# Adding the first heads' maxima to the transposed scores by matmuls, in a two-layer decoder on one core

## The chip, the core and the metric

The kernel runs on one core of one Trainium2 chip. The metric is the device time of one execution in microseconds (us); the median of several runs counts.

## The reference

Two decoder layers on x of 8 x 128 tokens x 128 features. Each layer is attention, cross attention and a mixture of experts, each with a residual and a layer norm after it. What matters here are the two self-attentions, with heads of width 8:

```
# layer 0: 16 heads, each with two queries and keys (c = 0, 1), differential attention
# layer 1: 16 heads in 8 pairs, causal
score = q @ k.T * 8 ** -0.5            # 128 x 128 for each of 8 sequences
attn  = softmax(score, axis=-1)        # row maximum subtracted, exp, divided by the row sum
y     = attn @ v
x     = layernorm(x + y @ Wout)
```

## The kernel before

**Stages.** The program is one instruction stream for each engine, tied by semaphores. Its stages are: projections and rotary tables of layer 0 (up to 34 us), attention A (layer 0, 16 heads, 34 to 111 us), cross attention, experts of layer 0, projections of layer 1, attention D (layer 1, 8 head pairs, causal, 216 to 269 us), cross attention with 16 heads, and the experts of layer 1 up to the end. A head below is one of the 16 steps of A or one of the 8 of D; each has 16 tiles of 128 x 128 scores (two columns c and 8 sequences b).

**Stacks.** Queries and keys are split in three bfloat16 parts each. The nine products of parts are made in one matmul by stacking: `queries_of[slot]` and `keys_of[slot]` hold 72 rows (`ROWS`: 3 x 3 x 8), read back from DRAM by `load_stacks` with four DMAs a head, into one of 8 slots (`RING`). Semaphore `stack[h % 4]` tells that head h has landed.

**What a head does.** Scores are made twice.

- `scores` (L600) multiplies queries by keys (72 rows) into banks 2 and 3, four tiles to a group g = 0 to 3; VectorE takes the negated row maxima of a group (`maxima`, L1384) and so frees the bank for the group after next.
- GpSimd splits the 16 maxima of each row in three bfloat16 parts (`split_maxima`, L486 to L492, semaphore `msplit`), TensorE transposes them to 48 x 128 (`head_maxima`, L632), ScalarE copies the result into `mT` (`copy_maxima`, semaphore `mc`).
- SyncE then moves `mT` by a DMA into rows 72 to 74 of the queries' stack (`move_maxima`, L368, semaphore `mrow`). Against these rows the keys' stack holds ones, so that
- `scores_t` (L613) makes the transposed scores with the maxima already subtracted, with 75 rows, into banks 4 and 5; ScalarE takes the exponential (`exponentials`), and
- `head_values` (L644) and `head_token` (L656) multiply by the values and transpose back.

In D each group of scores begins with one more matmul that adds the causal mask (L606, L619, 512 columns).

**Order.** TensorE's order is written out by hand in `heads` (L659). Heads 0 and 1 get their scores ahead, with `keep_busy` matmuls (L598, 128 x 512, results unused) in between; the transposition of head 0's maxima is placed inside head 1. Then come groups 0 and 1 of head 2, `keep_busy(8)`, and the steps: step n holds the transposed scores of head n, the scores of head n+2 (groups 2, 3) and n+3 (groups 0, 1), the maxima of head n+1, the values of head n-1. Steps 1 and 2 begin with `keep_busy(4)`. SyncE's order is: load stacks 0 to 3, then for each n: move the maxima of head n, load stack n+4.

Of the kernel before, what the change touches and what calls it, by code (L numbers as in the profile page):

```python
# [22 lines left out]
P = 128  # L23
# [18 lines left out]
RING = 8  # L42
AHEAD = FLIGHT = 4
LOADS = PARTS + 1
ONES_PAIR = 1.0019378662109375
EARLY_VALUES = 4
NEAR_VALUES = 3
# [59 lines left out]
def decoder_kernel(nc, d, out):  # L107
    with ExitStack() as ctx:
        def sb(name, shape, dt=F32):
            return ctx.enter_context(nc.sbuf_tensor(name, shape, dt))  # L110

        def sem(name):
            return ctx.enter_context(nc.semaphore(name))
# [3 lines left out]
        con = sb("con", [P, C_ALL])  # L117
        identb, trib, onesb, causS, causT, minusb = (
            sb(n, [P, P], BF16) for n in ("identb", "trib", "onesb", "causS", "causT", "minusb"))
        one = sb("one", [P, 1])  # L120
        xres = sb("xres", [P, B, P])
        racc = sb("racc", [P, B, P])
# [107 lines left out]
        def tiles(ap, n, w):  # L230
            return ap[:, 0:n * w].rearrange("p (a b) -> p a b", b=w)
# [3 lines left out]
        def over(ap, n):  # L235

            return ap.unsqueeze(1).to_broadcast([ap.shape[0], n, ap.shape[1]])
# [8 lines left out]
        def late_head(n, count):  # L246

            return isinstance(n, int) and n >= count
# [44 lines left out]
                self.y = sem(n + "_y")  # L293

        A, D = Heads("a", 0), Heads("d", NH // FLIGHT)
        ln_var, ln_rstd, ln_out, ln_tp, ln_xT = (sem("ln_" + n) for n in ("var", "rstd", "out", "tp", "xT"))
        resb = sem("resb")
        bkv, bkvc = sem("b_kv"), sem("b_kvc")
# [25 lines left out]
        def _(sp):  # L324
# [39 lines left out]

            def move_maxima(a, n, slot):

                sp.wait_ge(a.mc, n + 1)
                sp.dma_start(queries_of[slot][MROW:MROW + PARTS], mT[:, n % 2, :]).then_inc(a.mrow[n % FLIGHT], 16)  # L368

# [222 lines left out]
        def _(pe):  # L592
            mm = nc.tensor.matmul

            def keep_busy(count, at):

                for _ in range(count):
                    mm(bank(at), onesb[:], fill, start=True, stop=True)  # L598

            def scores(a, n, slot, g, causal):  # L600

                if not early(4 * n + g, 2):
                    pe.wait_ge(a.max, 4 * n + g - 1)
                o = bank(BANK_S + g % 2)
                if causal:
                    mm(tiles(o, 4, P), identb[:], over(causS[:], 4), start=True, stop=False)  # L606
                for k in range(4):
                    c, b = divmod(4 * g + k, B)
                    last = mm(o[:, k * P:(k + 1) * P], queries_of[slot][0:ROWS, c, b * P:(b + 1) * P],  # L609
                              keys_of[slot][0:ROWS, c, b * P:(b + 1) * P], start=not causal, stop=not causal or k == 3)  # L610
                last.then_inc(a.s, 1)

            def scores_t(a, n, slot, g, causal):  # L613

                if not early(4 * n + g, 2):
                    pe.wait_ge(a.exp, 4 * n + g - 1)
                o = bank(BANK_T + g % 2)
                if causal:
                    mm(tiles(o, 4, P), identb[:], over(causT[:], 4), start=True, stop=False)  # L619
                for k in range(4):  # L620
                    c, b = divmod(4 * g + k, B)
                    last = mm(o[:, k * P:(k + 1) * P], keys_of[slot][0:MROW + PARTS, c, b * P:(b + 1) * P],  # L622
                              queries_of[slot][0:MROW + PARTS, c, b * P:(b + 1) * P],
                              start=not causal, stop=not causal or k == 3)
                last.then_inc(a.st, 1)

            def head_maxima(a, n, slot):
# [31 lines left out]
            def heads(a, count, pair, causal):  # L659

                def step(n, slot):
                    ahead, second, third, before = ((slot + k) % RING for k in (1, 2, 3, -1))
                    if not late_head(n, count):
                        if n in (1, 2):
                            keep_busy(4, BANK_O + 1)
                        pe.wait_ge(a.mrow[n % FLIGHT], (a.turns + n // FLIGHT + 1) * 16)
                        scores_t(a, n, slot, 0, causal)
                        scores_t(a, n, slot, 1, causal)
                    if not late_head(n + 2, count):
                        scores(a, n + 2, second, 2, causal)  # L670
                    if not late_head(n + 1, count):
                        head_maxima(a, n + 1, ahead)
                    if not early(n, 1):
                        head_values(a, n - 1, before, pair, 0)
                    if not late_head(n + 2, count):
                        scores(a, n + 2, second, 3, causal)
                    if not early(n, 1):
                        head_values(a, n - 1, before, pair, 1)
                    if not late_head(n, count):
                        scores_t(a, n, slot, 2, causal)  # L680
                        scores_t(a, n, slot, 3, causal)
                    if not late_head(n + 3, count):
                        pe.wait_ge(a.stack[(n + 3) % FLIGHT], (a.turns + (n + 3) // FLIGHT + 1) * 16 * LOADS)
                        scores(a, n + 3, third, 0, causal)
                        scores(a, n + 3, third, 1, causal)
                    if not early(n, 1):
                        head_token(a, n - 1)

                for h in range(2):
                    pe.wait_ge(a.stack[h], (a.turns + 1) * 16 * LOADS)  # L690
                    for g in range(4):
                        scores(a, h, h, g, causal)
                        keep_busy(1 if causal else 2, BANK_O)
                        if h == 1 and g == 1:
                            head_maxima(a, 0, 0)
                pe.wait_ge(a.stack[2], (a.turns + 1) * 16 * LOADS)
                scores(a, 2, 2, 0, causal)
                scores(a, 2, 2, 1, causal)
                keep_busy(8, BANK_O)
                for n in range(count + 1):  # L700
                    step(n, n % RING)

# [93 lines left out]
            keep_busy(10, BANK_M0)  # L796
            pe.wait_ge(bkvc, 4)
            pe.wait_ge(fixed, 8)
            heads(A, NH, pair=False, causal=False)
            finish(A, 2, wproj0)  # L800
            keep_busy(10, BANK_T)
# [292 lines left out]
        def _(act):  # L1094
# [15 lines left out]
            def heads(a, count):  # L1110
                def exponentials(n, slot, g):
                    act.wait_ge(a.st, 4 * n + g + 1)
                    if g == 0 and not early(n, 2):
                        act.wait_ge(a.pv, n - 1)
                    fn(probs[:, slot % 2, 4 * g:4 * g + 4, :], tiles(bank(BANK_T + g % 2), 4, P), ACT.Exp).then_inc(a.exp, 1)

                def copy_maxima(n, slot):
                    act.wait_ge(a.mt, n + 1)
                    if not early(n, 2):
                        act.wait_ge(a.mrow[(n - 2) % FLIGHT], (a.turns + (n - 2) // FLIGHT + 1) * 16)  # L1120
                    fn(mT[:, slot % 2, :], maxima_bank[0:PARTS * 16, :], ACT.Copy).then_inc(a.mc, 1)

                def copy_outputs(n, slot):
                    act.wait_ge(a.pv, n + 1)
                    if not early(n, 1):
                        act.wait_ge(a.to, n)
                    fn(outT[:], bank(BANK_O + slot % 2), ACT.Copy).then_inc(a.ot, 1)

                def step(n, slot):
                    if not late_head(n, count):  # L1130
                        exponentials(n, slot, 0)
                    if not late_head(n + 1, count):

                        copy_maxima(n + 1, (slot + 1) % RING)
                    if not late_head(n, count):
                        exponentials(n, slot, 1)
                    if not early(n, 1):
                        copy_outputs(n - 1, (slot - 1) % RING)
                    if not late_head(n, count):
                        exponentials(n, slot, 2)  # L1140
                        exponentials(n, slot, 3)

                copy_maxima(0, 0)
                for n in range(count + 1):
                    step(n, n % RING)
# [225 lines left out]
        def _(dve):  # L1371
# [3 lines left out]
            def link(ins):  # L1375
                dch(ins)
                dch.wait()
# [103 lines left out]
            dve.wait_ge(lam_exp, 1)  # L1481
            link(tt(lams[:, 4:5], lams[:, 3:4], lams[:, 2:3], ALU.subtract))
            link(ts(lams[:, 5:6], lams[:, 4:5], -(0.8 - 0.6), None, ALU.add))
            heads(A, NH, finish_a)
            for half in range(2):
                dve.wait_ge(A.y, half + 1)
# [297 lines left out]
```

## Time and profile before

| | us |
|---|---|
| median of 3 runs | 510.82 |
| the runs | 511.9, 509.09, 510.82 |
| the profiled execution | 507.72 |
| its span, first to last instruction | 505.6 |

The profiled execution lies 3.1 us below the median of the runs; about 2 us of it lie around the span. The chain of work that ended last is 74% TensorE, 10% VectorE, 7% DMA and 4% ScalarE. The profile names TensorE's matmuls PE and its weight loads PEld. A matmul's row gives its start and a modelled length which contains the pipeline's depth, so matmuls that follow each other overlap in it; the distance from start to start is what one costs. The chain of work shows these costs added up without overlap.

### The profile page before, as it was taken

The numbers are of one execution on the slowest core, as the hardware profiler recorded it, in microseconds if no ns is written. First come the engines' busy times: TensorE is split into PE (matmuls) and PEld (weight loads), VectorE is DVE, ScalarE is ACT, GpSimd is POOL, SyncE is SP. The second block draws the span as 40 slices with busy tenths as digits, with TensorE's granted clock in tenths as the row PEclk, the third lists the DMA queues.
The fourth block names the chain that finished last, engine by engine and source line by source line (L and its number), as shares of the span: only waits on it lengthen the run. The fifth ranks groups of instructions, "written<-read, shape, count | busy, mean of one in ns | idle before, by whom it ended". The sixth has DMA issues, their size and how long they took to land.

```text
span 505.6 us, 11016 instructions
## 1 busy us (share of the span) xinstructions
PE 460.2 (91%) x4144; PEld 331.5 (66%) x4144; DVE 266.6 (53%) x682; ACT 237.7 (47%) x467; POOL 108.5 (21%) x227
## 2 busy tenths in 40 slices
PE   9698999988589998989998899998989999999993
PEld 3165777766345994346677678787866677677773
DVE  4725778716781537654534688876033422333236
ACT  2943667751231423404564588878305434433340
POOL 4202445423200012211111345444010000000001
PEclk9699999999959999989999999999999999999998
DMA  6866455150400000574101000100000011111111
GB/s 173 312 199 156 145 146 153 43 184 17 168 0 1 0 3 6 158 175 118 51 25 49 12 13 17 52 2 1 1 2 21 22 32 42 42 42 32 30 33 42
DMA packets 23307, 34.40 MB, mean 68 GB/s; under 512 B 7600, under 2 KB 16000, under 8 KB 23008
## 3 DMA queue, kind: packets, MB, share of 16 engines
q1 hardware_dynamic: 23264, 33.81, 22.7%
q8 instruction: 30, 0.49, 0.4%
q14 instruction: 13, 0.11, 0.1%
HBM read 28.26 MB, written 5.24 MB: 66 GB/s over the span
## 4 chain that ended last, share of the span: by engine, by line
PE 74%; DVE 10%; DMA 7%; ACT 4%; issue 2%; SPq 1%; POOL 1%; POOLq 0%; DVEq 0%; ACTq 0%
PE ps L1033 11%; PE ps L1050 11%; PE ps L644 4%; PE ps L622 4%; PE ps L609 4%; PE ps L956 3%; PE ps L980 3%; PE ps L598 3%; PE ps L1021 3%; PE ps L967 3%; PE ps L927 3%; PE ps L851 2%; ACT arena L1098 2%; DMA arena<-mT 2%; PE ps L885 2%; PE ps L656 2%
## 5 line engine op out<-in xcount | busy, mean ns | idle before, releaser
L1384 DVE TENSOR_REDUCE negm<-ps 128x4 f32<-128x512 f32 x96 | 64.0, 688 | 36.9 <-PE ps L609 34.7
L1098 ACT ACTIVATE arena<-ps,w1a 128x512 f32<-128x512 f32 x64 | 43.5, 687 | 58.9 <-PE ps L1033 57.8
L1707 DVE SCALAR_TENSOR_TENSOR racc<-ps,sm,racc 128x128 f32<-128x128 f32 x128 | 35.9, 344 | 63.2 <-PE ps L1050 63.1
L1098 ACT ACTIVATE probs<-ps 128x512 f32<-128x512 f32 (+1 forms) x100 | 56.4, 592 | 23.2 <-PE ps L622 22.3
L1050 PEld LDWEIGHTS ps<-w1a,arena 128*128 128x128 f32 x512 | 59.4, 192 | 7.2 <-issue 6.2
L1050 PE MATMUL ps<-w1a,arena 128*128 128x128 f32 x512 | 59.8, 275 | 0.8 <-DVE racc L1698 0.8
L1033 PE MATMUL ps<-xT,w1a 128*128 128x512 f32 x128 | 58.8, 601 | 1.4 <-ACT xT L1098 1.4
L1098 ACT ACTIVATE arena<-ps 128x512 f32<-128x512 f32 (+4 forms) x71 | 40.3, 592 | 35.5 <-PE ps L851 16.1
L533 POOL TENSOR_SCALAR rstd<-mv 128x4 f32<-128x4 f32 x12 | 2.7, 228 | 185.3 <-DVE mv L1430 185.3
L598 PE MATMUL ps<-onesb 128*128 128x512 bf16 x134 | 38.6, 417 | 3.0 <-DVE sm L1562 2.1
L1033 PEld LDWEIGHTS ps<-xT,w1a 128*128 128x128 f32 x128 | 23.1, 191 | 24.6 <-issue 22.2
L577 POOL TENSOR_TENSOR probs<-probs,rzE 128x480 f32<-128x480 f32 x32 | 30.9, 988 | 38.3 <-DVE rzE L1643 38.3
L644 PE MATMUL ps<-probs,vs 128*32 128x128 f32 x768 | 29.7, 278 | 0.7 <-issue 0.7
L1098 ACT ACTIVATE xT<-ps 128x512 f32<-128x512 f32 x10 | 6.0, 596 | 43.9 <-PE ps L729 43.8
L1098 ACT ACTIVATE outT<-ps 128x512 f32<-128x512 f32 x24 | 14.3, 597 | 18.3 <-PE ps L644 18.3
L1098 ACT ACTIVATE probs<-ps,negm 128x120 f32<-128x120 f32 x64 | 17.9, 368 | 10.5 <-DVE negm L1625 10.5
L598 PEld LDWEIGHTS ps<-onesb 128*128 128x128 bf16 x134 | 13.3, 105 | 14.4 <-issue 3.3
L1642 DVE TENSOR_REDUCE rzE<-probs 128x4 f32<-128x480 f32 x32 | 20.3, 635 | 3.8 <-ACT probs L1098 3.8
L1625 DVE TENSOR_REDUCE negm<-ps 128x4 f32<-128x480 f32 x32 | 19.2, 641 | 4.6 <-PE ps L956 4.6
L644 PEld LDWEIGHTS ps<-probs,vs 128*32 128x32 f32 x768 | 18.5, 109 | 4.5 <-issue 1.1
L486 POOL TENSOR_TENSOR mparts<-negm,zero 128x16 bf16<-128x16 f32 x24 | 5.3, 222 | 67.4 <-DVE negm L1384 67.4
L1098 ACT ACTIVATE near<-ps 120x512 f32<-120x512 f32 x32 | 17.5, 604 | 4.2 <-PE ps L967 4.2
(211 smaller groups left out, 816.8 us busy)
## 6 DMA issues: line engine op xcount, KB each, us to landing
stackA<-arena SPq DMA_DIRECT2D x12, 256.0 KB, 3.5
arena<-stackA SPq DMA_DIRECT2D x24, 96.0 KB
arena<-stackA SPq DMA_DIRECT2D x8, 288.0 KB
w1a<-in_w1a SPq DMA_DIRECT2D x1, 2048.0 KB, 8.7
w2a<-in_w2a SPq DMA_DIRECT2D x1, 2048.0 KB, 7.7
w1a<-in_w1b SPq DMA_DIRECT2D x16, 128.0 KB, 2.0
w1a<-in_w2b SPq DMA_DIRECT2D x16, 128.0 KB, 2.0
stackD<-arena SPq DMA_DIRECT2D x6, 256.0 KB
```

Of the source, the lines that this page charges most:

```text
L577: nc.gpsimd.tensor_tensor(weights, weights, along(rzE[:, slot, 4 * g:4 * g + 4], L), ALU.mult).then_inc(e_norm, 1)
L598: mm(bank(at), onesb[:], fill, start=True, stop=True)
L609: last = mm(o[:, k * P:(k + 1) * P], queries_of[slot][0:ROWS, c, b * P:(b + 1) * P], keys_of[slot][0:ROWS, c, b * P:(b + 1) * P], start=no ...
L622: last = mm(o[:, k * P:(k + 1) * P], keys_of[slot][0:MROW + PARTS, c, b * P:(b + 1) * P], queries_of[slot][0:MROW + PARTS, c, b * P:(b + 1 ...
L644: last = mm(bank(BANK_O + slot % 2)[32 * (b % 4):32 * (b % 4) + 32, col:col + P], vs[:, slot % 2, c if pair else 0, b, :], probs[:, slot % ...
L1033: mm(bank(BANK_S + u), w1s[:, slot, f * P:(f + 1) * P], xT[:, half * HALF:(half + 1) * HALF], start=True, stop=True).then_inc(g_up, 1)
L1050: last = mm(bank(banks + half)[:, k * P:(k + 1) * P], hid1[:, slot, f, b * P:(b + 1) * P], w2s[:, slot, f, :], start=f == 0, stop=f == F1 - 1)
L1098: return nc.scalar.activation(o, i, f, **kw)
L1384: nc.vector.tensor_reduce(negm[:, slot % 2, 4 * g:4 * g + 4], tiles(bank(BANK_S + g % 2), 4, P), AX.X, ALU.max, negate=True).then_inc(a.ma ...
L1625: nc.vector.tensor_reduce(negm[:, slot, 4 * g:4 * g + 4], tiles(bank(BANK_S + g % 2), 4, L), AX.X, ALU.max, negate=True).then_inc(e_max, 1)
L1642: link(nc.vector.tensor_reduce(r, probs[:, slot, 4 * g:4 * g + 4, 0:L], AX.X, ALU.add))
L1707: last = stt(racc[:, b, :], bank(banks + half)[:, k * P:(k + 1) * P], sm[:, 11, bass.ds(b * E1 + e, 1)], racc[:, b, :], ALU.mult, ALU.add)
```

## The change

For heads 0 to 2 of A and heads 0 and 1 of D (`direct`), the maxima don't go by DMA into the stack. The transposed scores of such a head use the 72 rows of the stacks alone, and after each tile a second matmul adds the maxima into the same tile: its stationary operand is one column of `tile_rows` (48 x 16, ones at rows t, t+16 and t+32 of column t) broadcast to 128 columns, its moving operand is `mT`, 48 x 128. That is 16 more matmuls for a direct head. TensorE waits for `mc` in place of `mrow`.

SyncE, for a direct head, waits until the head's first scores are made and issues no DMA, and goes on to load stack n+4. ScalarE's `copy_maxima` waits for the transposed scores of the head two before where that one was direct.

TensorE's order at the beginning of both attentions changes: groups 0 and 1 of head 2 and head 1's maxima stand in step 0 behind the first two groups of transposed scores, and `keep_busy(8)` is gone. VectorE builds `tile_rows` with two additions of pieces of the identity before attention A.

```diff
+DIRECT_A, DIRECT_D = 3, 2
+        tile_rows = sb("tile_rows", [PARTS * 16, 16], BF16)
+        A.direct, D.direct = DIRECT_A, DIRECT_D
+        def rows_moved(a, n):
+            skipped = (n % FLIGHT < DIRECT_A) + (n % FLIGHT < DIRECT_D if a is D else 0)
+            return (a.turns + n // FLIGHT + 1 - skipped) * 16
             def move_maxima(a, n, slot):
+                if n < a.direct:
+                    sp.wait_ge(a.s, 4 * n + 1)
+                    return
                 sp.wait_ge(a.mc, n + 1)
...
+                direct = n < a.direct
+                rows = ROWS if direct else MROW + PARTS
                 for k in range(4):
                     c, b = divmod(4 * g + k, B)
+                    tile = o[:, k * P:(k + 1) * P]
+                    last = mm(tile, keys_of[slot][0:rows, c, b * P:(b + 1) * P], queries_of[slot][0:rows, c, b * P:(b + 1) * P],
+                              start=not causal, stop=not direct and (not causal or k == 3))
+                    if direct:
+                        last = mm(tile, tile_rows[:, 4 * g + k:4 * g + k + 1].to_broadcast([PARTS * 16, P]), mT[:, n % 2, :],
+                                  start=False, stop=not causal or k == 3)
                 last.then_inc(a.st, 1)
...
-                        pe.wait_ge(a.mrow[n % FLIGHT], (a.turns + n // FLIGHT + 1) * 16)
+                        if n < a.direct:
+                            pe.wait_ge(a.mc, n + 1)
+                        else:
+                            pe.wait_ge(a.mrow[n % FLIGHT], rows_moved(a, n))
                         scores_t(a, n, slot, 0, causal)
                         scores_t(a, n, slot, 1, causal)
+                    if n == 0:
+                        head_maxima(a, 1, ahead)
+                        pe.wait_ge(a.stack[2], (a.turns + 1) * 16 * LOADS)
+                        scores(a, 2, second, 0, causal)
+                        scores(a, 2, second, 1, causal)
                     if not late_head(n + 2, count):
                         scores(a, n + 2, second, 2, causal)
-                    if not late_head(n + 1, count):
+                    if n > 0 and not late_head(n + 1, count):
                         head_maxima(a, n + 1, ahead)
...
-                pe.wait_ge(a.stack[2], (a.turns + 1) * 16 * LOADS)
-                scores(a, 2, 2, 0, causal)
-                scores(a, 2, 2, 1, causal)
-                keep_busy(8, BANK_O)
                 for n in range(count + 1):
                     step(n, n % RING)
...
+            pe.wait_ge(tables, 6)
             heads(A, NH, pair=False, causal=False)
...
-                        act.wait_ge(a.mrow[(n - 2) % FLIGHT], (a.turns + (n - 2) // FLIGHT + 1) * 16)
+                        if n - 2 < a.direct:
+                            act.wait_ge(a.st, 4 * (n - 1))
+                        else:
+                            act.wait_ge(a.mrow[(n - 2) % FLIGHT], rows_moved(a, n - 2))
...
+            dve.wait_ge(tables, 5)
+            link(tt(tile_rows[:], identb[0:48, 0:16], identb[0:48, 16:32], ALU.add))
+            tt(tile_rows[:], tile_rows[:], identb[0:48, 32:48], ALU.add).then_inc(tables, 1)
             heads(A, NH, finish_a)
```

## Rows read from the trace of the kernel before

**Rows 1.** The page's first part: busy us, share of the span, instructions of each engine.

```profile
PE 460.2 (91%) x4144; PEld 331.5 (66%) x4144; DVE 266.6 (53%) x682; ACT 237.7 (47%) x467; POOL 108.5 (21%) x227
```

**Rows 2.** Stretch: its us, busy PE, PEld, DVE, ACT, POOL, granted clock, DMA, GB/s.

```profile
56.00:104.00 48.00, 46.20 (x804) 35.17 (x804) 34.92 (x68) 34.92 (x73) 23.23 (x81) 1.00 0.39 113
...
216.00:224.60 8.60, 7.44 (x49) 4.20 (x49) 4.89 (x8) 0.27 (x1) 0.88 (x4) 0.80 0.76 184
```

**Rows 3.** Chain of work, start of attention A: start us, us, what.

```profile
33.90 7.35 DMA w1a<-stackA
...
41.92 1.73 PE ps L598 x8
...
44.82 2.42 DMA near<-mT
...
47.29 0.62 PE ps L622 x8
...
52.09 0.45 PE ps L622 x8
...
53.26 2.66 DMA w1a<-mT
...
55.97 0.62 PE ps L622 x8
```

**Rows 4.** Timeline, 34 to 42 us: start, us, engine, line, operation, [idle before <- releaser].

```profile
34.89 1.29 DVE L1384 TENSOR_REDUCE negm<-ps 128x4 f32<-128x512 f32 x2 [1.39 <-PE ps L609]
...
39.09 0.27 ACT L1098 ACTIVATE mT<-ps 48x128 bf16<-48x128 f32 x1 [5.97 <-PE ps L632]
...
39.88 0.60 PE L598 MATMUL ps<-onesb 128*128 128x512 bf16 x2
...
41.74 0.22 POOL L492 TENSOR_TENSOR mparts<-mres,mparts 128x16 bf16<-128x16 f32 x1
```

**Rows 5.** Chain of work inside the step of head 3.

```profile
56.59 0.23 PE ps L609 x4
...
57.55 0.33 PE ps L609 x4
```

**Rows 6.** Timeline of TensorE alone, the same stretch.

```profile
56.42 0.39 PE L609 MATMUL ps<-arena 72*128 72x128 bf16 x4
56.74 0.24 PE L632 MATMUL ps<-identb,mparts 128*48 128x128 bf16 x1
56.91 0.64 PE L644 MATMUL ps<-probs,vs 128*32 128x128 f32 x16
```

**Rows 7.** Timelines of TensorE at two other changes of shape, 16 and 64 rows.

```profile
395.24 1.02 PE L1033 MATMUL ps<-xT,w1a 128*128 128x512 f32 x2
...
395.67 0.59 PE L1033 MATMUL ps<-xT,w1a 128*128 128x512 f32 x1
396.19 0.37 PE L1078 MATMUL ps<-b2s,oT 16*128 16x128 f32 x1
...
299.38 0.61 PE L956 MATMUL ps<-w2a,arena 64*128 64x120 f32 x8
299.92 0.70 PE L927 MATMUL ps<-xT,arena 128*128 128x512 f32 x1
```

**Rows 8.** Chain of work: matmuls with a broadcast stationary operand (L857) and without.

```profile
161.66 1.78 PE ps L857 x16
163.45 1.79 PE ps L868 x16
```

**Rows 9.** Chain of work, start of attention D.

```profile
232.28 0.22 PE ps L619
...
238.66 0.22 PE ps L619
```

**Rows 10.** Timelines at the start of attention D.

```profile
224.67 0.38 PE L606 MATMUL ps<-causS,identb 128*128 128x512 bf16 x1
...
226.16 0.22 POOL L492 TENSOR_TENSOR mparts<-mres,mparts 128x16 bf16<-128x16 f32 x1
```

More of the change, by code:

```diff
@@ L619, in scores_t @@
                     mm(tiles(o, 4, P), identb[:], over(causT[:], 4), start=True, stop=False)
+                direct = n < a.direct
+                rows = ROWS if direct else MROW + PARTS
                 for k in range(4):
                     c, b = divmod(4 * g + k, B)
-                    last = mm(o[:, k * P:(k + 1) * P], keys_of[slot][0:MROW + PARTS, c, b * P:(b + 1) * P],
-                              queries_of[slot][0:MROW + PARTS, c, b * P:(b + 1) * P],
-                              start=not causal, stop=not causal or k == 3)
+                    tile = o[:, k * P:(k + 1) * P]
[4 more added lines that the diff above has]
+                                  start=False, stop=not causal or k == 3)
                 last.then_inc(a.st, 1)
```

## The prediction

> **What bounds the kernel now.** I read the page's first part, then the busy time by stretch, then the chain of work and the timelines at the two places that the change touches. TensorE is busy 91% of the span, the next engine 53% [rows 1]. Inside attention A, from 56 to 104 us, it is busy 46.2 of 48 us at the full clock [rows 2]: whatever is added to its order there is paid in full, and only at the beginning of each attention is there slack. The chain shows that slack. In A it runs through the landing of head 2's stack at 41.25 us (33.90 + 7.35), then the eight `keep_busy` matmuls (1.73 us), and head 1's transposed scores start at 47.29 behind a DMA of its maxima of 2.42 us; head 2's start at 52.09, head 3's at 55.97 behind another such DMA of 2.66 us [rows 3]. In D head 1's transposed scores start at 232.28 and head 2's at 238.66, both behind matmuls, not behind a DMA [rows 9]; the same eight `keep_busy` stand before head 0.
>
> **What the change removes.** It ends the waits for the moved maxima of five heads and the two `keep_busy(8)`. The most that this can give is, in A, the 0.95 us without work between the last `keep_busy` of head 1 (two from 39.88, some 0.215 apart, so done with issue at 40.3) and 41.25, the 1.73 us, and the two idle moments ahead of heads 1 and 3 (0.25 and 0.35 us, an estimate from the ends of the matmuls before them): 3.3 us [rows 3, 4]. In D it is the same eight matmuls, 1.73 us. Five small DMAs go from SyncE's queue, and stacks 4 to 6 are asked for earlier; no wait of TensorE for a stack behind head 2's stands in the chain, so I take nothing for that.
>
> **What it adds: 80 matmuls, 48 for A and 32 for D.** The question of the whole case is what one costs. A matmul of 72 rows that follows its like costs 0.057 us: four of L609 take 0.39 us with one of them 0.22 long, so three distances make 0.17 [rows 6]. Were the added one to cost the same, a direct head would cost 16 x 0.056 = 0.9 us more. The broadcast of its stationary operand costs nothing: 16 passes with one take 1.78 us, 16 without 1.79 [rows 8].
>
> But the added matmul has 48 rows, and it stands between two of 72. What happens where TensorE goes from the full array to a smaller piece of it can be read at four places. The transposition L632, with 48 columns, starts at 56.74, and the last L609 started at 56.42 + 0.17 = 56.59: 0.15 us in place of 0.057. From L632 to L644 it is 0.17 [rows 6]. Four L609 behind L644 take 0.33 us of the chain, behind their like 0.23 [rows 5]. For rows in place of columns there are two: L1078, with 16 rows, starts 0.52 us after an L1033, and these stand 0.43 apart (two take 1.02 with a length of 0.59); L927 starts 0.20 us after the last L956, of 64 rows, and these start two at a time and 0.11 apart (eight take 0.61 with a length of some 0.27, the last at 299.72) [rows 7]. All give 0.09 to 0.11 us for one change of shape, with 16 rows and with 64; a 48-row matmul lies between. The kernel's 72-, 75-, 96- and 128-row ones change among themselves for nothing.
>
> So a tile of a direct head costs 0.15 (into the small shape) + 0.17 (back) + 0.01 = 0.33 us against 0.056: **0.27 us more a tile, 4.3 us a head**. From below the term is 0.056 a tile (no change of shape at all), from above 0.37, if the 0.10 by which a group behind another shape is longer [rows 5] came once more on top of the distances. I take 0.27, from the bfloat16 rows with the same 128 moving columns.
>
> The Trainium skill ("TensorEngine Tiling (Array Packing)", Tiling Modes) says that a change of tiling mode drains TensorE, and it counts a contraction of up to 64 as one that a half-height tile takes; by it 48 rows are on the wrong side of the line, which no row here shows for exactly 48. It gives no price; by it the sum stays what the rows make it, and it speaks against this change.
>
> **Attention A step by step.** Now the first two groups of head 0 start at 40.3, since `mT` is there at 39.36 [rows 4]. Eight tiles x 0.33 bring TensorE to 42.9. Head 1's parts are split at 41.96 [rows 4]: no wait; L632 ends at 43.1, head 2's groups 0 and 1 (eight tiles, 0.45) at 43.6. Here the moved order makes a new wait: groups 2 and 3 need the banks that VectorE frees, and its two reductions take 1.3 us together [rows 4], from 43.4 to 44.7; so TensorE is at 44.9, after head 0's last eight tiles at 47.7, after head 3's two groups (0.45) at 48.1 and after `keep_busy(4)` (0.86) at 49.0, where head 1 starts: 1.7 us later than before. Head 1 took 52.09 - 47.29 = 4.8 us, now 9.1, to 58.1. Head 2 took 3.5 without its wait, now 7.8, to 65.9. Head 3's maxima still go by DMA, but they are transposed some 5 us before that and need 0.3 + 2.7 us. **A: 65.9 - 55.97 = +9.9 us.**
>
> **Attention D.** Head 0's first groups start at 224.67 [rows 10] and take 0.9 (with the mask matmuls) + 8 x 0.27 = 3.1, to 227.8; head 1's split is done at 226.4 [rows 10]. L632 0.17, head 2's two groups 0.9 (228.9), groups 2 and 3 behind VectorE to 230.3, head 0's last groups 3.1 (233.4), head 3's two 0.9, `keep_busy(4)` 0.86: head 1 starts at 235.1, +2.8. Head 1 costs 4.3 more. **D: +7.1 us**, and later heads keep their 75 rows and their pace.
>
> Edits taken at nothing: the two additions for `tile_rows` lie in 1.39 us in which VectorE had no work [rows 4], some 0.3 us if that cover were gone. ScalarE's new wait is for matmuls that its own last exponential needed. SyncE's new waits are for scores made microseconds earlier; behind them stand only stack loads, and heads 4 to 6 are not near.
>
> **The sum**: 507.7 (the profiled execution's own time) + 9.9 + 7.1 = 524.7. The median of the runs is 3.1 us above that execution, which gives 527.8. I predict 527.
>
> **Rivals.**
> - *The clock falls as well* (0.06). While shapes alternate, only 0.11 of each 0.33 us streams. Ahead of D, after idle time, the granted clock is 0.80 on average over 8.6 us, so it stood at the lower of its two levels for a part of them [rows 2]. Against it: between the groups stand dense matmuls. If it stood at the lower level for half of the 26 us of A's direct heads, of which some 60% streams (the rest is changes of shape), that part would take twice its time, 8 us more: 535.
> - *48 rows aren't a change of shape* (0.10). Then a tile costs 0.056 more. A: head 0's first groups end at 41.2, the wait for the split (41.96) and for VectorE hide half a microsecond, head 3 starts at 56.5, +0.5; D the same, +0.5. 508.7, or 511.8 by the median: no difference. For it: no row has exactly 48 rows; the Trainium skill ("TensorE: Matmul & The Clock Gate", Why this matters for your kernels) says that a single matmul with 32 rows takes the time of one with 128. Against it: both neighbours, 16 and 64 rows.
> - *Faster* (0.04): the 48-row matmul runs in the shadow of its neighbour and costs nothing. Then the chain gets shorter by what the waits allow, about 2.0 us in A (head 1 at 45.9 instead of 47.3, heads 2 and 3 each without their wait) and 1.3 in D: 504.4, 507.5 by the median. It decides for faster only below some 0.01 us a tile; nothing with 72 rows, which needs the array's whole height, suggests it.
>
> **How the numbers follow.** My forecast has 0.80; it and the clock rival are slower by over 0.5% (which is about what a measurement of this kernel can tell from no change): 0.86. The same: 0.10; faster: 0.04. With the smallest price for a change of shape (0.09 twice) the sum is 509 + 14 = 523, with 0.37 a tile it is 535. The range is 518 to 536; it leaves out the two rivals below and the worst of the clock's.
>
> **What would show each step.** Right: the added matmuls start 0.15 us after the 72-row ones and these 0.17 after them; head 3 of A starts near 66 us, head 2 of D 7 us later than before after the shift of A; no idle moment of TensorE on DMA for heads 0 to 3. Wrong: a distance of 0.056 (the second rival), the weight load of a 72-row matmul placed before the 48-row one ends, or a granted clock below 1 between 40 and 66 us. What would upset it most is a different rule for which row counts count as small.

## The result: 568 us, and a clock that stayed down

The changed kernel takes 568.38 us (median of 4 runs, 555.43 to 575.37) against 509.98 of the kernel before, a ratio of 1.0958 (95% interval 1.0864 to 1.1052; the ratio is made from the runs near each kernel's shortest, so it lies below that of the medians). The forecast was 527. The profiled execution took 561.64 us with a span of 559.2, 53.6 more than before. The direction was right, the size was a third of what came.

The page of the kernel after, its first part and the row of the granted clock (tenths of full speed in 40 slices), and the same clock row of the kernel before:

```profile
PE 515.9 (92%) x4207; PEld 365.8 (65%) x4208; DVE 268.9 (48%) x684; ACT 238.8 (43%) x467; POOL 108.5 (19%) x227
```

```profile
PEclk9695655558989599998779999999999999999997
```

```profile
PEclk9699999999959999989999999999999999999998
```

TensorE is still the engine that is busy all the time, 55.7 us more of it than in [rows 1]. The second row tells why: a slice is 14 us, and from the fourth to the ninth (42 to 126 us) the clock stands at five or six tenths, where the kernel before has nine. Busy time by stretch in the kernel after (columns as in [rows 2]):

```profile
34.00:44.60 10.60, 9.78 (x79) 5.61 (x78) 6.33 (x11) 1.62 (x4) 1.99 (x9) 1.00 0.77 170
44.60:65.10 20.50, 20.50 (x125) 11.11 (x126) 6.41 (x11) 4.33 (x8) 2.65 (x11) 0.50 0.33 74
65.10:68.50 3.40, 3.40 (x31) 1.97 (x33) 0.28 (x1) 0.71 (x2) 0.49 (x2) 1.00 0.00 0
76.10:129.90 53.80, 53.80 (x553) 42.63 (x551) 26.55 (x49) 23.55 (x48) 15.98 (x56) 0.50 0.30 89
258.90:324.40 65.50, 63.88 (x663) 39.63 (x664) 25.29 (x46) 24.00 (x48) 9.09 (x40) 0.87 0.25 67
```

and attention D in the kernel before:

```profile
216.70:269.50 52.80, 51.16 (x639) 34.03 (x640) 24.97 (x46) 23.70 (x48) 9.09 (x40) 0.97 0.31 83
```

Up to 44.6 us the clock is full. From there it is at its lower level, 1.2 GHz in place of 2.4, for 20.5 us. At 65.1 us, behind the four `keep_busy` matmuls ahead of head 2, it comes back. Head 2 begins with eight pairs of 72 and 48 rows (65.24 to 67.79), and at 68.5 us the clock falls again, although TensorE was busy all the time (3.40 of 3.40). From there it stays down until 129.9 us, again without an idle moment of TensorE (53.80 of 53.80). The row from 76.10 on is the surprise: no direct head is left there, only heads 3 and on, called the steady heads below. In D the clock falls four more times between 269 and 294 us, and the stage is 65.5 us long instead of 52.8.

The changes of shape themselves are where the prediction put them. Timeline of TensorE in the kernel after, in head 0 of A at the full clock, and in the same head at the lower one:

```profile
40.63 0.22 PE L639 MATMUL ps<-near 72*128 72x128 bf16 x1
40.78 0.23 PE L642 MATMUL ps<-mT,tile_rows 48*128 48x128 bf16 x1
40.94 0.23 PE L639 MATMUL ps<-near 72*128 72x128 bf16 x1
41.10 0.23 PE L642 MATMUL ps<-mT,tile_rows 48*128 48x128 bf16 x1
...
45.78 0.28 PE L642 MATMUL ps<-mT,tile_rows 48*128 48x128 bf16 x1
46.00 0.29 PE L639 MATMUL ps<-near 72*128 72x128 bf16 x1
46.22 0.28 PE L642 MATMUL ps<-mT,tile_rows 48*128 48x128 bf16 x1
```

0.15 or 0.16 into the small shape and 0.16 out of it, 0.32 a pair against the 0.33 of the forecast, where 72 rows behind 72 take 0.057 [rows 6]. At the lower clock the pair is 0.44. And the chain of work at the start of heads 3 and 4, which are no direct heads:

```profile
76.13 0.85 PE ps L639 x8
76.98 0.43 PE ps L623 x4
...
82.88 0.85 PE ps L639 x8
```

Four tiles take 0.43 where [rows 5] show 0.23. The head lasts 82.88 - 76.13 = 6.75 us; at the full clock such a head lasts 3.96 (the fifth experiment below shows one).

### The profile page after: what moved, and what is told of

It is laid out like the page before. It is cut to its first block, busy times and chain, and to the rows that moved or that the text cites. A ratio compares the mean times of both kernels' runs of the same rounds, so it can differ in the third digit from the quotient of the medians.

```text
span 559.2 us, 11141 instructions
## 1 busy us (share of the span) xinstructions
PE 515.9 (92%) x4207; PEld 365.8 (65%) x4208; DVE 268.9 (48%) x684; ACT 238.8 (43%) x467; POOL 108.5 (19%) x227
## 4 chain that ended last, share of the span: by engine, by line
PE 78%; DVE 11%; DMA 4%; ACT 2%; issue 1%; POOL 1%; SPq 1%; POOLq 0%; DVEq 0%; ACTq 0%
PE ps L1074 10%; PE ps L1057 10%; PE ps L639 7%; PE ps L663 6%; PE ps L623 6%; PE ps L612 3%; PE ps L980 3%; PE ps L1004 3%; PE ps L675 3%; PE ps L642 3%; PE ps L1045 3%; PE ps L991 3%; PE ps L951 2%; PE ps L875 2%; PE ps L909 2%; PE ps L620 2%
## 5 line engine op out<-in xcount | busy, mean ns | idle before, releaser
L663 PE MATMUL ps<-probs,vs 128*32 128x128 f32 x768 | 39.1, 341 | 0.7 <-issue 0.7
L663 PEld LDWEIGHTS ps<-probs,vs 128*32 128x32 f32 x768 | 23.2, 131 | 6.6 <-issue 3.3
L1122 ACT ACTIVATE outT<-ps 128x512 f32<-128x512 f32 x24 | 14.3, 597 | 30.3 <-PE ps L663 30.3
L1122 ACT ACTIVATE xT<-ps 128x512 f32<-128x512 f32 x10 | 6.0, 597 | 42.6 <-PE ps L752 42.5
L623 PE MATMUL ps<-arena 72*128 72x128 bf16 x192 | 22.2, 260 | 0.0
L612 PEld LDWEIGHTS ps<-onesb 128*128 128x128 bf16 x118 | 12.7, 113 | 14.2 <-issue 5.2
L675 PE MATMUL ps<-con,outT 128*128 128x128 f32 x96 | 19.8, 344 | 1.9 <-ACT outT L1122 1.9
```

The lines of the kernel that those rows point to most:

```text
L663: last = mm(bank(BANK_O + slot % 2)[32 * (b % 4):32 * (b % 4) + 32, col:col + P], vs[:, slot % 2, c if pair else 0, b, :], probs[:, slot % ...
L675: last = nc.tensor.transpose(bank(BANK_M1)[:, k * P:(k + 1) * P], outT[:, k * P:(k + 1) * P], ident)
L1122: return nc.scalar.activation(o, i, f, **kw)
```

## The experiments

Three explanations could be told apart. **A**: the changes of shape let the clock fall. **B**: the new order, with eight `keep_busy` matmuls less and new gaps. **C**: the added matmuls as such. And a second question: why does the clock stay down long after the last direct head? Comparisons are with runs of the kernel before on the same chip (medians 510.4, 510.5 and 509.4 us in the three groups).

**1. Same matmuls, no change of shape.**

```diff
-        tile_rows = sb("tile_rows", [PARTS * 16, 16], BF16)
+        tile_rows = sb("tile_rows", [ROWS, 16], BF16)
-        mT = sb("mT", [PARTS * 16, 2, P], BF16)
+        mT_all = sb("mT", [ROWS, 2, P], BF16)
+        mT = mT_all[0:PARTS * 16]
...
-   mm(tile, tile_rows[:, ...].to_broadcast([PARTS * 16, P]), mT[:, n % 2, :], ...)
+   mm(tile, tile_rows[:, ...].to_broadcast([ROWS, P]), mT_all[:, n % 2, :], ...)
...
+            link(nc.vector.memset(mT_all[:], 0.0))
```

> The changed kernel with its added matmuls made 72 rows high instead of 48: `mT` and `tile_rows` get 24 more rows of zeros, everything else (order, waits, the 80 added matmuls) stays. Theory: the loss comes from changing between 72 and 48 rows 160 times (0.10 us each, and only a third of the time streaming, which lets the granted clock fall). Then an added matmul starts 0.056 us after its neighbour, the clock stays at 1 through attention A, and the time is 508 to 513 us. Rival, the new order (no eight keep_busy matmuls, head 2's scores later) lets the clock fall: the clock still falls near 44 us and the time is above 540. Rival, the mere number of added matmuls: also above 520.

512.49 us, ratio 1.0048 (0.999 to 1.0106). Timeline of TensorE, head 0 of A:

```profile
40.78 0.22 PE L640 MATMUL ps<-near 72*128 72x128 bf16 x1
40.84 0.22 PE L643 MATMUL ps<-mT,tile_rows 72*128 72x128 bf16 x1
40.89 0.22 PE L640 MATMUL ps<-near 72*128 72x128 bf16 x1
...
42.48 0.24 PE L652 MATMUL ps<-identb,mparts 128*48 128x128 bf16 x1 [0.64 <-POOL mparts L507]
42.65 0.62 PE L624 MATMUL ps<-w1a 72*128 72x128 bf16 x8
43.83 1.21 PE L624 MATMUL ps<-w1a 72*128 72x128 bf16 x8 [0.56 <-DVE negm L1412]
```

Twenty-four rows of zeros take away 56 us of 58. An added matmul now starts 0.055 us after its neighbour, as the second rival of the prediction wanted for 48 rows; its 508.7 (511.8 by the median) is near what this kernel gives. That is in part luck, since its sum has the clock up throughout. C falls. The expectation missed one thing: the clock fell here too, for 7 us near 44 (0.79 on average over 40 to 56 us), behind the two idle moments in the rows (0.64 and 0.56 us), and came back at 50.7, behind the four `keep_busy` ahead of head 1.

```profile
40.00:56.00 16.00, 14.78 (x169) 11.49 (x168) 8.38 (x14) 5.50 (x11) 3.38 (x15) 0.79 0.55 135
56.00:100.00 44.00, 43.15 (x767) 33.63 (x764) 33.28 (x63) 31.68 (x66) 21.43 (x75) 1.00 0.44 127
```

**2. The order alone.** `DIRECT_A, DIRECT_D = 0, 0`.

> The changed kernel with no direct head at all: the maxima of every head go by DMA into the stack as before, and only the new order is left (head 1's maxima and head 2's first scores inside step 0, no eight keep_busy matmuls). Theory (changes of shape): the time is within 2 us of before, 508 to 512, clock at 1 through attention A. Rival (order): the clock falls in A and the time is above 540.

515.83 us, ratio 1.01 (1.0055 to 1.0145). It is neither the 508 to 512 of A nor the 540 of B: the order costs 5 us by itself. TensorE's timeline shows the place:

```profile
45.17 1.03 PE L639 MATMUL ps<-near 75*128 75x128 bf16 x8 [3.83 <-DMA near<-mT]
```

Without direct heads, step 0 waits 3.83 us for the moved maxima, which head 2's scores and `keep_busy(8)` used to fill, and the clock falls near 44 for 10 us.

**3. Fewer changes of shape.** The four 48-row matmuls of a group stand together behind its four of 72 rows; in A the `start` flag goes to the group's first alone.

```diff
-                    if direct:
-                        last = mm(tile, ...)
+                if direct:
+                    for k in range(4):
+                        last = mm(o[:, k * P:(k + 1) * P], ..., start=False, stop=k == 3)
```

> The changed kernel with the same 80 matmuls of 48 rows, but the four of a group together behind the group's four of 72 rows: 2 changes of shape a group instead of 8. Theory: a direct head costs 16 x 0.056 + 8 x 0.10 = 1.7 us more, five heads 8.5, of which 4.6 are covered as in the prediction: 513 to 516 us at an unfallen clock. Rival (the number of added matmuls, or 48 rows in themselves, lower the clock): above 530.

518.76 us, ratio 1.0148 (1.011 to 1.0186), 3 us above the range that I gave; in the profiled execution the clock fell near 43 for 17 us, and one of the four runs took 554.19, as if it had not come back there. A quarter of the changes, with the same 80 matmuls of 48 rows, takes away 50 us of 58. So it is not the 48 rows in themselves.

**4. Dense matmuls behind the direct heads.** `keep_busy(20, BANK_O + 1)` ahead of head 3 of A.

> The changed kernel with 20 more keep_busy matmuls (128 x 512) ahead of head 3 of attention A, behind its last direct head. Theory: once the clock has fallen, the steady heads of A run at the lower level only because nothing in them lifts it; 20 dense matmuls cost 4.3 to 8.6 us and the heads behind them go back from 6.75 to 3.96 us each: 525 to 545 us. Rival (the steady heads hold the clock down by themselves whatever went before, or something else slows them): 565 to 580 us.

547.94 us, ratio 1.0713 (1.0654 to 1.0772): for 20 matmuls more it is 20 us shorter than the changed kernel by the medians, 12 by the ratios (1.0713 against 1.0958), and 3 us beyond the upper end of the expectation. The chain of work there:

```profile
77.18 0.85 PE ps L675 x4
78.03 6.21 PE ps L612 x20
84.24 0.45 PE ps L639 x8
...
88.00 0.23 PE ps L639 x4
```

Twenty matmuls of 512 columns take 6.21 us, begun at the lower clock (0.43 each) and ended at the full one (0.22), and the head behind them runs at full pace: eight tiles in 0.45 instead of 0.85. The clock rises at 81.7 us. So the steady heads run well at the full clock if something lifts it. They also kept it through a wait of 1.51 us for moved maxima, which ended at 113.54 us.

**5. The kernel before, with its sixteen `keep_busy` matmuls a stage taken out.** No added matmul, no new order.

> The kernel before, with the 16 keep_busy matmuls (8 ahead of head 0, 4 each ahead of heads 1 and 2) taken out of both attentions; no added matmul, no new order. Theory: the clock falls near 44 us while TensorE waits for maxima, and once it is down the steady heads of A, which are the same instructions as in the kernel before, do not bring it back; they run at 6.75 us a head instead of 3.96 up to about 125 us: 530 to 545 us. Rival (the steady heads bring the clock back within a few heads, and it was the added matmuls that kept it down): 508 to 518 us.

Its 11 runs lie between 504.86 and 539.34 us, with a median of 515.37: the median lies in the rival's range, two of the runs lie in the theory's, and neither describes this kernel. This spread is the kernel's own and can't be left aside; the ratio, 0.9949 (0.9892 to 1.0005), is made from the shortest runs and doesn't show it. The profiled execution (526.13 us) is one of the slower ones. Its chain of work:

```profile
83.52 0.85 PE ps L622 x8
...
90.27 0.85 PE ps L622 x8
...
99.78 0.57 PE ps L644 x16
100.35 0.55 PE ps L622 x8
...
101.80 0.24 PE ps L622 x4
...
105.76 0.23 PE ps L622 x4
```

Here the very instructions of the kernel before run at 6.75 us a head (90.27 - 83.52), at the lower clock from 44.6 us on, and then, with nothing different around them, at 3.96 (105.76 - 101.80) from 99.2 us on. This answers the second question: the steady heads of A keep the clock up if it is up (one exception stands in experiment 8), and do not reliably raise it if it is down. Here the lower level lasted into head 8; the shortest executions show a mean clock of 0.96, the longest 0.88, and that makes 35 us between two executions of one program.

**6. `keep_busy(8)` back ahead of head 0, all else as changed.**

> The changed kernel with the eight keep_busy matmuls back, ahead of head 0's transposed scores. Theory (changes of shape let the clock fall by themselves): the clock falls some microseconds later than at 44 us, still within the direct heads of A, and stays down behind them: 550 to 575 us. Rival (the missing eight matmuls are what lets the clock fall, the changes of shape cost their 0.10 us each and no more): the clock stays at 1 in A and the time is 522 to 532 us.

567.04 us (560.17 to 576.17) against 510.54. The clock fell at 48.8 instead of 44.6 us and stayed down until 123.9. So the eight missing matmuls are not the main cause: they put off the fall by 4.2 us, of which 1.7 are their own time. The other part of B, the order itself, is tried in experiment 9.

**7. One direct head in A and none in D**, and **8. two in D and none in A.**

> The changed kernel with one direct head in A and none in D. Theory: the clock falls near 44 us as in every kernel with the new order, but keep_busy(4) ahead of heads 1 and 2 bring it back since no changes of shape follow: 4.3 us for the head on top of the order alone (515.8), so 515 to 521 us. Rival (one direct head is enough to keep the clock down through A): above 535.

> The changed kernel with no direct head in A and two in D. Theory: on top of the order alone (515.8) D costs what it costs in the changed kernel, whose attention D is 12.7 us longer than before (65.5 against 52.8), of which some 7 are changes of shape and the rest short falls of the clock: 525 to 531 us. Rival (D is only slow because of what A did before it): 516 to 523 us.

517.35 us (ratio 1.0134, 1.0045 to 1.0222) and 527.25 us (1.0312, 1.0234 to 1.0389), both inside the range, the second for a reason that its profile doesn't bear out. One direct head adds 1.5 us to the order alone, less than its 4.3; that fits with the wait for the moved maxima (3.83 us in experiment 2), which goes with it. By the medians D's two direct heads cost 11.4 us on top of the order alone. The profiled execution divides its 18.2 us above that of experiment 2 (spans of 529.5 and 511.3) in another way. Two stretches of it, the steady heads of A and the whole of D but its start:

```profile
69.10:101.00 31.90, 31.88 (x342) 24.95 (x342) 14.79 (x27) 14.22 (x30) 9.73 (x34) 0.52 0.32 96
237.00:294.40 57.40, 55.38 (x653) 35.48 (x652) 23.46 (x46) 24.00 (x48) 9.09 (x40) 1.00 0.24 64
```

In A, where no head is direct, TensorE waits 1.36 us for moved maxima up to 69.1 us, the clock falls at 69.8 and stays down for 31 us, and D begins 11.1 us later than in experiment 2 (233.1 against 222.0). D itself, from its first matmul to the transposes behind its last head, takes 61.3 us, in the kernel before 54.2: 7.1 us more, at the full clock. So the changes of shape do not always bring the clock down, and an idle moment alone can bring it down for longer than experiments 1 and 2 show. The other three executions (524.25 to 528.37) were not profiled.

**9. The direct heads in the old order.**

> The direct heads (48 rows, three in A, two in D) in the order of the kernel before, with its eight keep_busy matmuls; none of the reordering. Theory (the changes of shape are what lets the clock fall and stay down): 550 to 575 us as in the changed kernel. Rival (order and added matmuls are needed together): 520 to 535 us.

551.44 us, ratio 1.0709 (1.0617 to 1.0801). The changes of shape, with every `keep_busy` and without the reordering, give 42 of the 58 us by the medians, 36 of 49 by the ratios. The order adds the rest, though the runs of the two kernels overlap (543.35 to 570.43 here, 555.43 to 575.37 there). The profiled execution (570.43 us) shows no idle moment of TensorE in the 5.2 us ahead of its first fall:

```profile
41.50:46.70 5.20, 5.20 (x37) 2.94 (x38) 1.43 (x4) 0.60 (x1) 1.11 (x5) 1.00 0.78 191
```

Its first eight pairs stand from 43.65 to 46.05 us, and the clock falls at 46.8. It comes back at 67.3, behind `keep_busy(4)`, and falls again at 70.7 behind the first eight pairs of head 2, as in the changed kernel.

**10. The 72-row kernel with its two gaps filled**, three `keep_busy` in each.

```diff
                     if n == 0:
+                        keep_busy(3, BANK_O)
                         head_maxima(a, 1, ahead)
...
                         scores(a, 2, second, 1, causal)
+                        keep_busy(3, BANK_O)
```

> The 72-row variant (first experiment) with three keep_busy matmuls ahead of head 1's maxima and three behind head 2's first scores, where TensorE stood idle for 0.86 and 0.78 us in step 0 of A. Theory: the fall of the clock near 44 us in every kernel with the new order comes from these two gaps; filled, it stays at 1 and A is 1 to 3 us shorter than in the 72-row variant (512.5): 508 to 511 us. Rival (the fall has nothing to do with the gaps): 511 to 515 us, clock down near 44 us.

510.41 us, ratio 1.0016 (0.9987 to 1.0045). Ten of the twelve runs lie between 507.63 and 511.83 us; the other two took 603.83 and 780.08. Two of the 23 runs of the kernel before in the same group took 768.54 and 1567.28, so such a run needs none of the edits. The expectation's 0.86 and 0.78 us count from the start of the matmul before; the profile's idle times are 0.64 and 0.56. The clock over 40 to 56 us, against 0.79 in experiment 1:

```profile
40.00:56.00 16.00, 15.80 (x234) 11.76 (x233) 9.69 (x16) 7.32 (x16) 4.50 (x19) 1.00 0.55 134
```

So in the 72-row kernel the fall belongs to the gaps, or to the lack of six matmuls of 512 columns; the two weren't separated, and each kernel has one profile. For the 48-row kernels this isn't shown: the changed kernel has only the second gap (0.56 us), and the kernel of experiment 9 falls with none. What was meant as a gain, no DMA wait for three heads, is now free of both its faults and is worth nothing that can be measured.

**11. The same without `keep_busy(4)` ahead of heads 1 and 2.**

> As the filled 72-row variant, and without the four keep_busy matmuls ahead of each of heads 1 and 2, in both attentions: a direct head has no DMA to wait for, so nothing has to be bridged. Theory: 0.86 us x 2 in A and in D less if the clock stays up, 505 to 508 us, faster than the kernel before. Rival (those matmuls are what keeps the clock up, as their removal from the kernel before spread its times over 505 to 539): a spread of the runs of more than 10 us, median above 511.

Thirteen runs between 505.68 and 540.13 us, median 514.15: the rival. Five of them lie between 505.7 and 507.5, the theory's own range and below every run of the kernel of experiment 10; four lie above 536. The ratio, again from the shortest runs, is 0.9939 (0.99 to 0.9978). Of its profiled execution (540.13 us):

```profile
55.69 0.22 PE L640 MATMUL ps<-w1a 72*128 72x128 bf16 x1 [1.72 <-issue]
...
40.00:56.00 16.00, 14.08 (x221) 10.81 (x220) 9.66 (x16) 7.34 (x15) 5.38 (x22) 1.00 0.70 152
56.00:100.00 44.00, 44.00 (x467) 35.05 (x464) 22.54 (x41) 20.06 (x41) 12.86 (x44) 0.52 0.30 93
```

A full clock over heads 0 and 1, then a fall at 57.7 us and no way back until 132.8. Ahead of the fall stands a pause of 1.72 us inside a group of head 2, at a place where the program waits for nothing and where the removed matmuls did not stand; what caused it isn't known. What the runs show is this: with the `keep_busy(4)`, which look like pure cost in a chain of work (0.86 us each), ten of twelve times lie within 4.2 us of each other, and without them thirteen spread over 34. By which step they do it isn't shown.

## Why the prediction was wrong

**What bounds the kernel, and the price of an added matmul: right.** Each change of shape costs 0.09 to 0.10 us at 48 rows, as at 16 and 64 [rows 7]; a pair is 0.32 against the forecast 0.33, and the broadcast operand costs nothing [rows 8]. At the full clock the ledger also holds in place: head 0's first two groups ended at 43.2 us (forecast 42.9), head 1's maxima needed no wait, and VectorE held up head 2's third group by 0.56 us. D's forecast of 7.1 us is what D costs where the clock stays up (experiment 8's profile). The rule of the Trainium skill that a change of tiling mode drains TensorE ("TensorEngine Tiling (Array Packing)", Tiling Modes) fits this: by the trace a change costs time, and 48 rows count as small. That what costs it is a drain, no run here shows. The sentence that a matmul of 32 rows takes the time of one of 128 ("TensorE: Matmul & The Clock Gate", Why this matters for your kernels), which stood behind a rival, speaks of a matmul by itself. Between 72-row neighbours one of 48 rows adds 0.26 us, one of 72 rows 0.055 (experiment 1).

One bound of the prediction is added up wrongly: with the smallest price (0.09 twice and 0.056) 80 matmuls cost 18.9 us, 14.3 with the 4.6 that are covered, and 510.8 + 14.3 makes 525, not 523. Nothing hangs on it.

**The ledger from 44.6 us on: wrong by the clock.** Against before (spans): head 3 of A starts at 76.13 in place of 55.97, +20.2, where the sum said +9.9; the other 10.3 us are the direct heads at the lower level. Heads 3 to 10 follow at 6.75 instead of 3.96 us: 8 x 2.79 = 22.3. Together 42.5, and D begins 42.2 us later than before (258.9 against 216.7). D takes 65.5 instead of 52.8: +12.7 for a forecast of 7.1, with the clock falling four times. What is left, -1.3 us, lies behind D. Of the 53.6 us, 17 are what the forecast gave to the added matmuls, with its waits and savings; the other 36 or so are put down to the clock, an estimate by difference.

**The steps that failed** are two sentences. "Later heads keep their 75 rows and their pace" took the pace for a property of the instructions; heads 3 to 10 of A ran at 6.75 us instead of 3.96, 22.3 us that no term of the sum holds. And the clock rival had the mechanism and the wrong size in both numbers: a chance of 0.06, and a price of 8 us because I let the low clock end with the direct heads and even then granted it half of them, where the difference above leaves some 36. Its argument against itself, "between the groups stand dense matmuls", fell with the profile itself, where the clock falls in head 0 and again in head 2 with these matmuls in place. Experiment 5 adds that the steady heads do not bring it back with any certainty. What the rows of before could have told is that they hold no steady head at the lower level, so that the price of a fall was open at the top; the bound should have been both attentions with all that streams in them at twice its time, tens of us more, and the range should have reached there.

**The new order: its effect on the clock was taken at nothing.** I had reckoned the waits behind it and not what the gaps do to the clock. It costs 5 us without direct heads (experiment 2), of which a part is the wait of 3.83 us that direct heads don't have. With them it is 17 us by the medians of experiment 9 and the changed kernel, whose runs overlap.

**Faster, and the 48 rows as no change of shape**: both fell. The second has the right price for an added matmul only once the rows are made 72.

**What stays open.** Why the steady heads sit on the edge (when they come back differs from one execution to the next, experiment 5) was not separated further: their own changes of shape at L632 and L644 [rows 5] are a candidate, but none was taken out. Nor is it known which idle moments matter. With no added matmul the clock fell behind waits of 3.83 us (experiment 2), of 1.39 and 1.74 (experiment 5) and of 1.36 (experiment 8), the latter for 31 us; it did not fall behind 0.82 and 0.66 us in the kernel before or behind 1.51 in experiment 4. Why D's direct heads bring it down in the changed kernel and not in experiment 8 is open too. How much of D's 12.7 us is clock in each execution differs, and only single profiles show it.

## What to carry to other kernels

Count the changes of matmul shape before adding a small matmul between large ones: pad its contraction with zero rows to the height of its neighbours, or group by shape. Wherever an edit thins out TensorE's stream, price the lower clock for the whole stage that follows and not only for the edited part, and ask what in that stage would lift it again. Filler matmuls that a chain of work shows as plain cost may hold the clock of everything behind them: take several executions of a kernel without them before believing the best one.

## What was not expected of the hardware

- The instructions of a stretch don't settle its granted clock: in one execution the same heads ran at the lower level from 56 to 99 us without one idle moment of TensorE, and from 99.2 on at the full one (experiment 5). Behind 20 matmuls of 512 columns, begun at 78.0 us, it was up from 81.7 (experiment 4).
- At the lower clock a pair of 72 and 48 rows takes 0.44 us against 0.32; two tiles of one shape 0.21 against 0.11. The cost of a change of shape there is 0.11 us, nearly what it is at the full clock.
- A stationary operand broadcast from one column costs what any other costs, in bfloat16 too: 0.055 us from start to start (experiment 1).
